# Two engines' queues re-ordered inside a chunk, and the last rstd taken from GpSimd to ScalarE and VectorE

## The reference, cut to what matters

```python
h = _ln(x, pw_g[pathway_ids], pw_b[pathway_ids])
h = _ln(h, cp_g[compartment_ids], cp_b[compartment_ids])
t = _ln(x, tm_g[time_steps], tm_b[time_steps])
m = x + _mlp_ln(memory_state, ...)[:, None, :]     # n, r alike
s = _ln(x, ms_g[scale_type], ms_b[scale_type])
w = softmax(aw)
cat = concatenate([w[0]*h, w[1]*t, w[2]*m, w[3]*n, w[4]*r, w[5]*s])
out = x + _ln(silu(cat @ int_W1 + int_b1) @ int_W2 + int_b2, int_g, int_be)
```

## Time and profile before

| | before |
|---|---|
| median of 3 runs | 950.84 us |
| all three | 950.84, 952.48, 950.79 us |
| profiled execution, its own time | 952.21 us |
| span of its trace, first to last instruction | 950.5 us |
| TensorE busy | 923.2 us |
| VectorE busy | 825.8 us |
| ScalarE busy | 326.0 us |
| GpSimd busy | 449.8 us |

### The profile page before, as it was taken

How to read it: one execution, slowest core, us unless ns; L and a number is a source line. 1 busy time by engine, 2 the same in 40 slices (tenths; PEclk the granted TensorE clock), 3 DMA queues, 4 the chain that set the end, 5 groups by cost and what they waited for, 6 DMA issues and landing times.

```text
span 950.5 us, 13455 instructions
## 1 busy us (share of the span) xinstructions
PE 923.2 (97%) x4166; PEld 745.4 (78%) x4166; DVE 825.8 (87%) x1199; ACT 326.0 (34%) x415; POOL 449.8 (47%) x576
## 2 busy tenths in 40 slices
PE   7999999999999999999999999999999999999997
PEld 6767887878888787887878878787887878788785
DVE  6899898898889889898889988889888988989855
ACT  5835224242332514224242332424233251432411
POOL 6355463643636454363644435355363645436122
PEclk9999999999999999999999999999999999999999
DMA  9984667648475674757657475774847667485432
GB/s 327 353 296 142 207 170 254 168 127 247 125 235 162 192 217 114 241 131 254 177 148 231 141 241 133 244 175 124 253 122 243 156 190 219 113 249 125 125 88 65
DMA packets 99618, 178.75 MB, mean 188 GB/s; under 512 B 10128, under 2 KB 49040, under 8 KB 95632
## 3 DMA queue, kind: packets, MB, share of 16 engines
q1 hardware_dynamic: 44656, 96.07, 29.0%
q0 software_dynamic: 22976, 66.07, 28.8%
q10 hardware_dynamic: 31968, 16.39, 5.9%
HBM read 145.75 MB, written 32.75 MB: 188 GB/s over the span
## 4 chain that ended last, share of the span: by engine, by line
DVE 35%; issue 34%; PE 13%; POOL 11%; ACT 3%; DMA 2%; DVEq 1%; POOLq 1%; ACTq 0%; SPq 0%
DVE yst L1096 4%; DVE y_sb L1093 4%; DVE y_sb L1112 4%; DVE xc L1014 3%; DVE r_sb L1175 3%; DVE v_ring L1059 3%; PE hid_ps L1567 3%; PE hid_ps L1568 3%; PE hid_ps L1569 3%; POOL pw_rows L619 3%; DVE y_sb L1084 2%; POOL pw_rows L612 2%; POOL frs L541 2%; DVE fst L1128 2%; DVE cat_lo L1064 2%
## 5 line engine op out<-in xcount | busy, mean ns | idle before, releaser
L1567 PE MATMUL hid_ps<-cat_hi,w_hi 128*128 128x512 f32 x1008 | 397.1, 394 | 14.1 <-DVE cat_lo L1064 14.1
L1568 PE MATMUL hid_ps<-cat_lo,w_hi 128*128 128x512 f32 x1008 | 393.1, 390 | 0.0
L1569 PE MATMUL hid_ps<-cat_hi,w_lo 128*128 128x512 f32 x1008 | 392.9, 390 | 0.0
L1567 PEld LDWEIGHTS hid_ps<-cat_hi,w_hi 128*128 128x128 f32 x1008 | 189.5, 188 | 66.3 <-DVE cat_lo L1064 21.5
L1569 PEld LDWEIGHTS hid_ps<-cat_hi,w_lo 128*128 128x128 f32 x1008 | 189.6, 188 | 39.9
L1568 PEld LDWEIGHTS hid_ps<-cat_lo,w_hi 128*128 128x128 f32 x1008 | 189.7, 188 | 38.4
L612 POOL DMA_INDIRECT pw_rows<-pw,path_now x64 | 77.2, 1206 | 91.6 <-DVE y_sb L1112 75.4
L619 POOL DMA_INDIRECT pw_rows<-cp,class_now x64 | 93.4, 1459 | 36.8 <-issue 17.3
L633 POOL DMA_DIRECT2D r_sb<-x x60 | 57.3, 955 | 106.4 <-DVE r_sb L1175 103.3
L853 ACT ACTIVATE z_sb<-hid_ps,batch_bias 128x512 f32<-128x512 f32 x64 | 43.8, 691 | 168.9 <-PE hid_ps L1569 168.9
L835 ACT ACTIVATE cat_hi<-v_ring 128x1024 fp32r<-128x1024 f32 x30 | 31.9, 1062 | 154.1 <-DMA v_ring<-h_turned 154.1
(11 more groups left out here) (187 smaller groups left out, 1414.4 us busy)
## 6 DMA issues: line engine op xcount, KB each, us to landing
x_sb<-xp SPq DMA_DIRECT2D x16, 1024.0 KB, 5.2
out<-r_sb SPq DMA_DIRECT2D x63, 256.0 KB, 2.0
xc<-xT SPq DMA_DIRECT2D x15, 1024.0 KB, 6.9
h_turned<-y_sb ACTq DMA_DIRECT2D x60, 256.0 KB, 6.5
r_sb<-x POOLq DMA_DIRECT2D x60, 256.0 KB, 4.6
v_ring<-h_turned SPq DMA_DIRECT2D x60, 256.0 KB, 3.3
stats_bc<-token_stats SPq DMA_DIRECT2D x15, 512.0 KB, 5.6
ids_sb<-ids SPq DMA_DIRECT2D x16, 256.0 KB, 5.3
```

The costliest lines, as they stand in the source:

```text
L1567: pe.matmul(acc, w1_hi[:, k, cols], hi, start=start, stop=False)
L1568: pe.matmul(acc, w1_hi[:, k, cols], lo, start=False, stop=False)
L1569: return pe.matmul(acc, w1_lo[:, k, cols], hi, start=False, stop=stop)
```

## The change

Three things are changed. First, in VectorE's queue for chunks 2 to 15, `ts_mult(b, 0)`, `ts_mult(b, 1)` and `ts_low(b, 0)` stand ahead of `y_norm(b, 2)` and `y_norm(b, 3)`; both `hidden_low` come earlier; the four `y_turn` stand together behind `ts_low(b, 1)`; `ts_mult(b, 2)` and `ts_mult(b, 3)` follow them. Chunks 0 and 1 are re-ordered in a like manner. Second, in ScalarE's queue `ts_high(b, 0)` and `ts_high(b, 1)` stand ahead of `y_hat(b, 2)` and `y_hat(b, 3)`, and `hinges(b, 3)` ahead of `h_write(b)`. Third, the factor of the very last output tile comes from a square root on ScalarE, a reciprocal and one Newton step on VectorE.

```diff
-            for t in range(TT):
+            for t in range(TT - 1):
                 out_rstd(BATCHES - 1, t)
...
             def first_chunk():
                 w_high(4)
+                ts_high(0, 0)
                 xhat_copy(1)
                 w_high(5)
-                ts_high(0, 0)
...
                     hidden_high(b - 1, 1)
+                    ts_high(b, 0)
+                    ts_high(b, 1)
                     y_hat(b, 2)
                     y_hat(b, 3)
-                    ts_high(b, 0)
-                    ts_high(b, 1)
                     hinges(b, 2)
+                    hinges(b, 3)
                     h_write(b)
-                    hinges(b, 3)
                     ts_high(b, 2)
                     ts_high(b, 3)
...
+            act.activation(last_cols[:, 0:1], eps_col[:, 0:1], ACT.Sqrt).then_inc(root_tabled, 1)
+            act.wait_ge(faggr, TT * BATCHES)
+            act.activation(last_cols[:, 1:2], fmv[:, TT - 1, 1:2], ACT.Sqrt, bias=eps_col[:, 0:1]).then_inc(last_root, 1)
...
+                dve.tensor_tensor(fve[:, t:t + 1], fmv[:, t, 1:2], eps_col[:, t:t + 1], ALU.add).then_inc(last_var, 1)
                 dve.scalar_tensor_tensor(o_sb[:, t % 2, :], second_ps[t], fmv[:, t, 0:1], g_bc,
                                          ALU.subtract, ALU.mult).then_inc(fnum, 1)
...
+                dve.reciprocal(about, last_cols[:, 1:2]).then_inc(last_step, 1)
...
+                dve.scalar_tensor_tensor(off, about, about, fve[:, t:t + 1], ALU.mult, ALU.mult).then_inc(last_step, 1)
...
+                dve.tensor_scalar(rest, off, -0.5, 1.5, ALU.mult, ALU.add).then_inc(last_step, 1)
...
+                dve.tensor_tensor(frs[:, t:t + 1], rest, about, ALU.mult).then_inc(frs_done, 1)
...
-                class_rows()
                 nets_norm()
+                class_rows()
...
                 else:
+                    y_norm(b, 0)
+                    y_norm(b, 1)
+                    ts_mult(b, 0)
+                    ts_mult(b, 1)
+                    ts_low(b, 0)
+                    hidden_low(b - 1, 0)
+                    y_norm(b, 2)
+                    y_norm(b, 3)
+                    hidden_low(b - 1, 1)
+                    ts_low(b, 1)
                     for t in range(TT):
-                        y_norm(b, t)
-                    hidden_low(b - 1, 0)
-                    ts_mult(b, 0)
-                    y_turn(b, 0)
-                    ts_mult(b, 1)
-                    y_turn(b, 1)
-                    ts_low(b, 0)
-                    y_turn(b, 2)
-                    y_turn(b, 3)
-                    ts_low(b, 1)
+                        y_turn(b, t)
                     ts_mult(b, 2)
-                    hidden_low(b - 1, 1)
                     ts_mult(b, 3)
                     ts_low(b, 2)
```

More of the change, by code:

```diff
@@ L149, in build @@
         frs = sb("frs", [P, TT])
+        last_cols = sb("last_cols", [P, 5])
         net_g = sb("net_g", [NR, D])
@@ L299, in build @@
         last_stored = sem("last_stored")
+        root_tabled = sem("root_tabled")
+        last_root = sem("last_root")
+        last_var = sem("last_var")
+        last_step = sem("last_step")
         last_lo_done = sem("last_lo_done")
@@ L895, in first_chunk @@
                 w_high(9)
+                ts_high(0, 2)
                 nets_silu()
+                ts_high(0, 3)
                 w_high(10)
                 w_high(11)
-                ts_high(0, 2)
                 w_high(12)
@@ L903, in first_chunk @@
                 w_high(15)
-                ts_high(0, 3)
                 for t in range(TT):
@@ L1155, in last_stats @@
                 dve.wait_ge(out_ready, n - 2)
+                if t < TT - 1:
+                    dve.scalar_tensor_tensor(o_sb[:, t % 2, :], second_ps[t], fmv[:, t, 0:1], g_bc,
+                                             ALU.subtract, ALU.mult).then_inc(fnum, 1)
+                    return
+                dve.tensor_tensor(fve[:, t:t + 1], fmv[:, t, 1:2], eps_col[:, t:t + 1], ALU.add).then_inc(last_var, 1)
                 dve.scalar_tensor_tensor(o_sb[:, t % 2, :], second_ps[t], fmv[:, t, 0:1], g_bc,
                                          ALU.subtract, ALU.mult).then_inc(fnum, 1)
+                about, off, rest = [last_cols[:, i:i + 1] for i in range(2, 5)]
+                dve.wait_ge(last_root, 1)
+                dve.reciprocal(about, last_cols[:, 1:2]).then_inc(last_step, 1)
+                dve.wait_ge(last_step, 1)
+                dve.wait_ge(last_var, 1)
+                dve.scalar_tensor_tensor(off, about, about, fve[:, t:t + 1], ALU.mult, ALU.mult).then_inc(last_step, 1)
+                dve.wait_ge(last_step, 2)
+                dve.tensor_scalar(rest, off, -0.5, 1.5, ALU.mult, ALU.add).then_inc(last_step, 1)
+                dve.wait_ge(last_step, 3)
+                dve.tensor_tensor(frs[:, t:t + 1], rest, about, ALU.mult).then_inc(frs_done, 1)
             def last_sum(t):
@@ L1289, in first_chunk @@
                 w_low(4)
+                ts_low(0, 0)
                 w_low(5)
-                ts_low(0, 0)
                 ts_mult(0, 1)
@@ L1295, in first_chunk @@
                 ts_low(0, 1)
-                class_columns(True)
-                y_mul(0, 0)
                 ts_mult(0, 2)
@@ L1300, in first_chunk @@
                 w_low(9)
+                ts_mult(0, 3)
+                ts_low(0, 2)
+                class_columns(True)
                 dve.wait_ge(tables_ready, 1)
-                y_mul(0, 1)
-                y_mul(0, 2)
-                y_mul(0, 3)
-                ts_low(0, 2)
+                for t in range(TT):
+                    y_mul(0, t)
+                ts_low(0, 3)
                 w_low(10)
@@ L1309, in first_chunk @@
                 y_add(0, 0)
-                ts_mult(0, 3)
                 y_add(0, 1)
-                ts_low(0, 3)
                 y_add(0, 2)
@@ L1326, in first_chunk @@
                 h_low(0, 1)
+                nets_norm()
                 class_rows()
-                nets_norm()
                 x_low(1, 0)
```

## The result

The changed kernel takes **967.99 us** (median of 965.15, 967.99 and 969.87), beside 951.55 for the kernel before in the same comparison. The ratio is 1.0169, with a 95% interval from 1.0135 to 1.0203: 12.8 to 19.3 us slower, 16.1 by the ratio itself. One more run of the changed kernel had a mean granted TensorE clock of 0.557, against 0.986 to 0.993 in the others, and took 1545.36 us; it is left out of the median and the ratio. The profiled execution is the one of 965.15, 12.9 us over the profiled one of before.

What follows compares the result with a forecast made beforehand. VectorE's chunk of 56.5 us, waits included, was taken as the bound. Loop +12.7, head start -3.15 and start -1.0 gave +8.5; with tail +0.6 and landing +2.4, +11.5 on 950.84: 962.3 us, range 952.5 to 973.

Steps and rivals of the forecast that it cites:

- VectorE sets the period, TensorE follows: Loop chunks: VectorE with its waits for ScalarE and GpSimd takes 56.5 us, TensorE at 55.45 follows.
- The hold of ScalarE makes two new waits, +0.98 us a chunk: Loop: VectorE waits 0.55 us before the first `ts_low` and 2.67 before the third, replacing the hinge wait of 2.18.
- Nothing behind it, the same instructions with the same neighbours, gives it back: Rest of each loop chunk, behind the third `ts_low`: the loss of 0.98 us stays whole.
- its term of 0.2 us a chunk: At `y_mul(b + 1, 0)`: later landing of the h writes leaves 0.6 us slack; +2.4 us in all.
- the sooner load of `xT`: Loop: `ts_mult(b, 3)` ends sooner, so this load starts sooner, which speaks against a landing wait in every chunk.
- The sum over the loop: Loop chunks 2 to 14: 13 by 0.98 us, +12.7, with landing waits of 0.2 us per chunk put separately.
- Head start of 3.15 us: `ts_low(b, 0)` starts at 488.05 instead of 491.20, a gain counted once, at `ts_low(15, 0)`.
- Chunks 0 and 1 give 1.0 us: Program start: moved `ts_mult` fill VectorE's idle 2.43 us in chunk 0, part is lost again; -1.0, bounds 0 and 2.4.
- Tail +0.6: Last output tile: four small dependent instructions make the last sums start later, +0.6 us, bounds +0.2 and +1.0.
- (1): Loop: the wait is removed and TensorE becomes the bound, 14 to 16 us saved, 936 us; chance 0.13.
- (2): Loop: landing of the h writes becomes a second wait in every chunk, 972 to 975 us; chance 0.2.
- The rule weighed: ScalarE's `h_write`: by the skill it would be free soon after the last `y_turn`; the trace showed 4.04 us of issuing.

Runs made afterwards that it cites:

- the better order: Changed loop with the four `y_turn` right behind the last `y_norm`, then `hidden_low`, `ts_low`, `ts_mult` and two `x_stats`; start and tail as before: 933.97 us, ratio 0.9820.
- the kernel with the turns early: Kernel before with the change's loop orders, but the four `y_turn` directly behind the last `y_norm`: 945.35 us, ratio 0.9955.
- the loop alone: Kernel before with only the change's new VectorE and ScalarE orders for chunks 2 to 15: +16.6 us by its ratio.
- `xT` behind the reads: Kernel before with the change's loop orders, and SyncE's load of `xT` moved behind the two reads of `h_turned`: 958.93 us, ratio 1.0083.
- `h_write` last: Kernel before with the change's loop orders, but `h_write` behind `ts_high(b, 3)` in ScalarE's queue: 964.43 us, ratio 1.0139.
- both orders of SyncE's queue: Kernel before with only the new chunks 0 and 1, small nets' weight loads ahead of chunk 1's loads, in the second their vectors too: 958.11 and 955.79 us.
- `y_mul` back: Kernel before with only the new chunks 0 and 1, but class columns and chunk 0's four `y_mul` where they stood: 950.45 us, ratio 0.9995.
- tail alone: Kernel before with only the last tile's factor by root and Newton step: -1.5 us against the kernel before.

## Why the prediction came out as it did

The forecast was +11.5 us and 962.3; measured are +16.1 by the ratio and 967.99, slower as forecast and within the range of 952.5 to 973, but above the likeliest range of 958 to 967. The terms below are read from the profiled execution, which is 12.9 us over that of before.

*VectorE sets the period, TensorE follows.* Right. With VectorE's waits gone (the better order) the period is 55.27 us, where the prediction read 55.45 us of TensorE's work.

*The hold of ScalarE makes two new waits, +0.98 us a chunk.* Right in its mechanism and place, too high in size. Both waits are there (35.7 us over 28), the old one is gone, and the stretch from the first `y_norm` to the third `ts_low` grew by 0.60. The term took 4.87 us from the last `y_turn` to ScalarE's next operation, with an issue of 4.04 in it; the issue in the chunk shown now takes 3.66, and the whole 4.4. That the late `y_turn` causes the longer of the two waits is shown by the kernel with the turns early, which takes 21 us less.

*Nothing behind it, the same instructions with the same neighbours, gives it back.* Here the prediction was wrong: something gives back, and something adds. The second `h_low` adds 1.27 us a chunk, for the read of `h_turned` is late for it, and 0.96 of it returns at the third `out_sum`, where VectorE had waited for GpSimd's factor. (The profile puts most of that wait to "issue", but in the chunks looked at VectorE starts 0.09 us behind the factor each time.) The prediction noticed that the landing loses cover of 1.8 us (2.78 - 0.98), but followed it only to its first reader, `y_mul`, and not on to the read, `h_high` and `h_low`. `y_mul` itself waits no more than before. So its term of 0.2 us a chunk was about the size of what came (1.27 - 0.96 = 0.31), at another place, which is luck.

The prediction counted the sooner load of `xT` as a help for the landing; the landing stayed at 15 us behind the last `y_turn`, so it was neither help nor harm. What the load costs by standing beside the writes at all, 2.2 us of landing, was in the kernel before too.

What the prediction left out is the load for the residual: released by `out_sum`, it now goes ahead of the last read, and that read takes 6.0 us. In the kernels whose loop has `y_turn` where it stood, this load is issued 1.4 to 1.8 us behind the last read, which takes 4.1 to 4.2; in the loop alone it is 0.8 ahead and 6.0. With `xT` behind the reads it is again 1.7 behind, with 4.6 and no wait; with `h_write` last it is 3.2 ahead, and the read takes 4.4. So the reads are slow where the two overlap, but no run moves that load alone: that it is the cause is argued and not shown.

*The sum over the loop.* 0.60 + 1.27 - 0.96, and -0.01 for the rest, make 0.90 us over 12 periods, 10.7 in all, where the prediction had 0.98 + 0.2 over 13, 15.1. The profiled execution is the fastest of its kind; the other two took 3 to 5 us more, and the loop alone has a period of 58.02 us in its profile, +1.40. The second wait does not make the difference, 15.8 us over 12 there and 15.9 over the loop chunks here. What does, in part, is what comes back: VectorE's idle time before all `out_sum` was 29.0 us before (19.8 put to "issue" and 9.2 to GpSimd), and is 14.0 here but 22.6 in the loop alone, where `y_mul` also waits 2.6 us for the writes. Why GpSimd's factor comes sooner in one than in the other is open.

*Head start of 3.15 us.* Borne out: from the last `turn_stats` to `ts_low(15, 0)` pass 38.20 us before and 35.05 in the kernel with `xT` behind the reads, 3.15 less, and its span is 4.3 us longer where its last `turn_stats` is 7.4 late.

*Chunks 0 and 1 give 1.0 us.* Wrong in sign: +5.9 and -0.5. The prediction looked at VectorE's idle time, which the moved `ts_mult` did fill, and not at what the moved `y_mul` release. Putting them back takes all of it away. Why 2.85 us of delay cost 5 us is only argued: the loads are issued closer together (the load of x to that of `xT` 3.9 us apart, where it was 7.9), the DMA engines are busy for 8 and 9 tenths from 24 to 72 us, by the page after, and both orders of SyncE's queue that were run kept the loss. Closeness alone is not enough, as with `y_mul` back the two loads are 4.2 us apart at no loss.

*Tail +0.6.* Right on VectorE (1.54 against 0.94 us) and wrong for the end, which comes 1.8 us sooner behind the sums. The kernels with the old tail (before, loop alone, better order) end 5.0 us behind the start of the sums, those with the new one 3.1 to 3.2. The trace's record of GpSimd's closing drain says why: it lasts 5.45 us in each of them, and begins together with GpSimd's last operation. Before it runs from 944.83 to 950.28, and the span ends at 950.5: this drain was the last thing that the program waited for, as SyncE was through at 948.4. With the last rstd off GpSimd it starts at 940.77 (tail alone), is over at 946.22, and the store ends the span at 948.3.

*The numbers.* 8.5 + 0.6 + 2.4 was 11.5 us; the profiled execution has 12.9. The term for the start was -1.0 and came as +5.4. The 13 loop chunks were to add 15.1 and added 11.8: 10.7 over the twelve periods, and 1.1 in chunk 1's end and from the last `turn_stats` to `ts_low(15, 0)`, where a second `h_low` waits. The head start of 3.15 came as it was put, and the tail as -1.2 instead of +0.6. Errors of both signs cancel in it, so that a sum off by 1.4 us is luck, with one term off by 6.4. Of the rivals, (1) fell as the hold stayed at 3.6 us in the mean of the loop chunks, above the 3.3 at which it decides; (2) came in a weaker form at `h_low`, and in full only where `h_write` was moved last.

*The rule weighed.* The Trainium skill ("DMA: Bandwidth & Descriptors", section "Issuing engines are not separate DMA queues") calls a sequencer's time for a DMA usually small "relative to the DMA itself", and so read this case's trace agrees: in the chunk shown one DMA of h takes 0.31 to 1.49 us of ScalarE, and 5.2 to 12.0 us from its issue to its landing. The prediction was wrong to read in it that ScalarE would be free soon. Four such issues in a row take 3.66 us, 4.8 us pass in which ScalarE computes nothing, and what they have to be small against is VectorE's 2.66 us of `ts_mult` behind the last `y_turn`. In these traces that is what the loop's order turns on.

## What to carry to other kernels

When an instruction moves, follow what it releases, not only what it waits for, and follow it to the last reader. Here `y_mul` frees a buffer for a load and starts gathers, `y_turn` opens the way to a write, a read and two more operations, and the time was lost there. Where one engine stands still to issue DMAs, place the release of that issue ahead of the longest work of the other engine that needs nothing from it: the loop order built on this was worth 17 us here, and the one that had it the other way cost 16. When the path runs through a transfer, ask what runs beside it: with 1 MB moved out of the way of the writes they landed 2.2 us sooner and half the loop's loss was gone, while letting that 1 MB go 4.6 us sooner beside them changed nothing in when the last write landed.
